# Three gathers in flight instead of two between two expert layers

## The reference

```
routed = sum over the 6 chosen experts k of  w[token, k] * expert_k(norm(x))[token]
x = x + routed + shared(norm(x))                       # layer 0 mixture
idx, w = small products of norm(x); s = sum(g[idx] * w) # lookup
x = x + s * (column sums of W_out) + b_out
probs = softmax(norm(x) @ gate_w.T); top 2 experts per token, then that mixture
```

## Time and profile before

| | us |
|---|---|
| median of three runs | 896.84 (895.16 to 898.3) |
| the profiled execution's own time | 900.07 |
| its span, first to last instruction | 898.3 |
| PE busy | 686.2 (76%) |
| DVE busy | 639.4 (71%) |
| ACT busy | 453.0 (50%) |
| POOL busy | 438.7 (49%) |
| DMA_INDIRECT of L1373, the gathers, 96 | 95.1 busy, 49.8 idle before them |

### The profile page before, as it was taken

How to read it: one execution, slowest core, us unless ns; L and a number is a source line. 1 busy time by engine, 2 the same in 40 slices (tenths; PEclk the granted TensorE clock), 3 DMA queues, 4 the chain that set the end, 5 groups by cost and what they waited for, 6 DMA issues and landing times.

```text
span 898.3 us, 17392 instructions
## 1 busy us (share of the span) xinstructions
PE 686.2 (76%) x5945; PEld 405.3 (45%) x5945; DVE 639.4 (71%) x1333; ACT 453.0 (50%) x620; POOL 438.7 (49%) x674
## 2 busy tenths in 40 slices
PE   4799999999999999714989999615244541899992
PEld 2422223223222233303889997312213311799991
DVE  5899998999899989862767643548688863344442
ACT  4778887888888888501434443101011011455550
POOL 4140002361255216576767774677766664255552
PEclk9999999999999999956999999955555555899997
DMA  7999999999999201253977663111111110133336
GB/s 243 290 319 282 314 295 297 311 296 287 273 341 367 119 3 50 69 140 103 271 231 211 168 176 100 45 42 46 55 57 39 52 58 26 33 52 50 53 44 156
DMA packets 83479, 142.91 MB, mean 159 GB/s; under 512 B 10736, under 2 KB 75728, under 8 KB 81888
## 3 DMA queue, kind: packets, MB, share of 16 engines
q1 hardware_dynamic: 57744, 118.07, 44.2%
q0 software_dynamic: 12784, 17.40, 8.1%
q10 hardware_dynamic: 12864, 6.33, 2.5%
HBM read 116.57 MB, written 101.34 MB: 243 GB/s over the span
## 4 chain that ended last, share of the span: by engine, by line
PE 55%; DMA 14%; DVE 10%; issue 7%; POOL 6%; ACT 6%; SPq 2%; POOLq 0%; ACTq 0%; DVEq 0%
PE PS L641 13%; DMA GB<-y_scratch,slotc 8%; PE PS L626 7%; PE PS L968 7%; PE PS L615 7%; PE PS L978 3%; PE PS L779 3%; ACT PB L1102 3%; PE PS L766 3%; PE PS L768 3%; DMA XP<-slots_scratch 3%; POOL slots_scratch L1316 2%; PE PS L754 2%; POOL slots_scratch L1391 2%; DVE routed L1767 1%
## 5 line engine op out<-in xcount | busy, mean ns | idle before, releaser
L1613 DVE TENSOR_SCALAR PS<-PS 128x1024 f32<-128x1024 f32 x244 | 289.6, 1228 | 14.1 <-PE PS L615 10.1
L1102 ACT ACTIVATE PB<-PS 128x1024 f32<-128x1024 f32 x224 | 227.8, 1025 | 46.8 <-PE PS L626 40.1
L641 PE MATMUL PS<-PB,VS 128*32 128x256 f32 x2048 | 164.2, 393 | 0.1
L1373 POOL DMA_INDIRECT GB<-y_scratch,slotc x96 | 95.1, 991 | 49.8 <-DMA GB<-y_scratch,slotc 34.8
L1316 POOL DMA_INDIRECT slots_scratch<-XN,slot x96 | 92.8, 967 | 52.8 <-ACT PB L1102 29.3
L615 PE MATMUL PS<-QS,KP 64*128 64x512 bf16 (+1 forms) x576 | 98.9, 359 | 9.0 <-ACT PB L1102 6.0
L626 PE MATMUL PS<-QM,KP 64*128 64x512 bf16 (+1 forms) x576 | 100.1, 362 | 2.2 <-DVE PS L1613 2.1
L1417 POOL DMA_INDIRECT sums_scratch<-YO,XG x39 | 60.7, 1556 | 60.0 <-DVE YO L1981 57.2
L968 PE MATMUL PS<-XTT,WB 128*128 128x128 f32 x624 | 77.8, 279 | 0.0
L968 PEld LDWEIGHTS PS<-XTT,WB 128*128 128x128 f32 x624 | 74.6, 196 | 0.1
L626 PEld LDWEIGHTS PS<-QM,KP 64*128 64x128 bf16 x576 | 25.1, 93 | 103.8 <-issue 49.9
(11 more groups left out here) (289 smaller groups left out, 1316.3 us busy)
## 6 DMA issues: line engine op xcount, KB each, us to landing
y_scratch<-YP SPq DMA_DIRECT2D x80, 128.0 KB, 2.3
slots_scratch<-slots_scratch SPq DMA_DIRECT2D x1, 8768.0 KB, 32.7
W0GU<-in_w0gu SPq DMA_DIRECT2D x1, 6144.0 KB, 48.1
XP<-slots_scratch ACTq DMA_DIRECT2D x80, 64.0 KB, 2.6
XP<-slots_scratch SPq DMA_DIRECT2D x80, 64.0 KB, 2.6
W1GU<-in_w1gu SPq DMA_DIRECT2D x8, 512.0 KB, 3.9
W0D<-in_w0d SPq DMA_DIRECT2D x1, 3072.0 KB, 16.8
XG<-slots_scratch SPq DMA_DIRECT2D x39, 68.5 KB, 1.9
```

Source lines behind the costliest of these rows:

```text
L641: last = mm(PS[32 * j:32 * j + 32, at:at + HALF], VS[:, n, g * HG + j, :], PB[u // 2 % 3][:, 2 * (j % 2) + j // 2, q], start=(n == 0 and h ...
L1102: A(PB[u // 2 % 3][:, 2 * hp:2 * hp + 2, :], pair_banks(u).rearrange("p (j q) -> p j q", j=2), ACT.Exp).then_inc(sem("exp_done"), 1)
L1373: gp.indirect_dma_start(GB[:, t, k, :], None, y0_dram.rearrange("b p d -> (b p) d"), bass.IndirectOffsetOnAxis(ap=slotc[:, t, k:k + 1], ax ...
L1613: TS_(pair_banks(u), pair_banks(u), 4.0, 0.0, ALU.mult, ALU.max).then_inc(sem("relu_done"), 1)
```

## The change

One constant. The semaphores `gathered0`, `gathered1` become `gathered0`, `gathered1`, `gathered2`; gather g waits for gather g - 3; `combined` waits on three semaphores with 2 gathers of each tile on each, instead of two with 3 on each. Nothing else differs.

```
-        IN_FLIGHT = 2
+        IN_FLIGHT = 3
...
                     if g >= IN_FLIGHT:
                         pool.wait_ge(sem(f"gathered{g % IN_FLIGHT}"), 16 * (g // IN_FLIGHT))
...
                 for g in range(IN_FLIGHT):
                     dve.wait_ge(sem(f"gathered{g}"), 16 * (TOP0 // IN_FLIGHT) * (t + 1))
```

## The result

The changed kernel takes 890.05 us (median of 7 runs, 887.54 to 893.88) against 896.84 for the kernel before (7 runs, 894.5 to 900.23): 6.8 us less, a ratio of 0.9919 with a 95% interval of 0.99 to 0.9939. Run once more beside the last experiments it gave 892.4 against 900.98, 0.9909 (0.9884 to 0.9934). The forecast was 891.0, in a range of 887.5 to 895.8.

A forecast was written before the change was run, and what follows sets the result against it. POOL's gathers were taken to set the ends of stretches A and B, DVE those of C and D. Gains of 3.3 + 2.5 = 5.8 us off the median 896.84 gave 891.0 us, range 887.5 to 895.8.

The forecast's parts named there:

- The price of a gather: On POOL between the expert layers: 1.245 us (0.942 held plus 0.30) with three in flight, against 1.365 with two.
- the rival by which landings stretch: Gathers land one behind another, landings stretch to 4 us, pace stays 1.365: 896.8 us; chance 0.08.
- A: First stretch between expert layers, 45.37 us, ending at DVE's wait for POOL's factor; 30 gathers, 3.3 us gain, range 1.6 to 5.1.
- B: Second stretch, 36.65 us, also ending with DVE waiting for POOL's factor; 24 gathers, 2.5 us gain.
- C and D: Third and fourth stretches, 37.97 and 36.12 us; POOL waits for DVE's moments at their ends, so no gain.
- The stall of 1.62 us at the 18th gather: In A at 581.40: POOL idles 1.92 us in place of 0.30 on nothing visible; the extra 1.62 was kept.
- four tosses against L1766: In A, gathers starting together with DVE's L1766 may be held, 0.8 to 0.9 us each; two hits of four taken.
- The step-through: POOL's gathers in B followed against L1766 in the times of before: 3.1 or 1.9 us earlier, 3.7 with no hit.
- the first rival: Other two-input DVE instructions also hold gathers, all four hits in A: gain 1.5 to 2.5 us, 894.8; chance 0.14.
- the toss: In B the 18th gather starts 0.08 us ahead of an L1766 and may slip by or be held.
- The slower rival: Gathers hold DVE's L1766, 12 of them, 0.7 us each: 8.4 us lost against 5.8 gained, 899.4; chance 0.06.
- the prediction's best case: No gather held in A or B: 5.1 + 3.7 = 8.8 us gained, 888.0; chance 0.14 as a rival.

The follow-up runs named there:

- the last experiments: Changed kernel with four gathers of chunk 2, in place of six, ahead of the last pair of scalings of B: 891.01 us against 900.98 for the kernel before.

## Why the prediction was right

- **The price of a gather** (1.245 for 1.365 us) and **the landing** that doesn't grow (2.5): as forecast; the rival by which landings stretch fell with the first profile. A landing was felt once after all, the longest of 3.8, for 0.57 us of idle time in D, where POOL has time to spare.
- **Which stretches pay**: A and B pay, C and D don't. The run with three in flight for C and D alone (1.0006) shows it, where the shares of the chain of waits would have promised 5 us.
- **A: 3.3 forecast, 6.2 measured**, more than the 5.1 that the prediction gave for no hit at all. Two terms were mis-sized. The stall of 1.62 us at the 18th gather was kept, as if it belonged to that gather; it runs from a landing, and with three in flight most of it is hidden. And of four tosses against L1766 two hits at 0.85 were counted, where one gather was held by 0.44: 1.26 less. 3.3 + 1.62 + 1.26 = 6.2. The tosses themselves were misread: only the last L1766 of A, at 586.60, began with a landing, and the gather that started 0.1 us ahead of it slipped by. The other three began right behind L1757, which waits for PE, so it is the pace of PE and DVE that decides which gather they meet; the one of 573.57 began inside the second of them. POOL's row beside the last L1766, then DVE's rows:

```profile
586.50 0.94 POOL L1373 DMA_INDIRECT GB<-y_scratch,slotc  x1 [0.30 <-issue]
```

```profile
572.58 0.69 DVE L1757 TENSOR_TENSOR X<-X,PS 128x512 f32<-128x512 f32 x1 [3.28 <-PE PS L815]
573.18 0.95 DVE L1766 TENSOR_TENSOR GB<-GB,wtok 128x768 f32<-128x768 f32 x1
...
586.60 0.96 DVE L1766 TENSOR_TENSOR GB<-GB,wtok 128x768 f32<-128x768 f32 x1 [3.15 <-DMA GB<-y_scratch,slotc]
```

- **B: 2.5 forecast, 1.8 measured** between these two profiles, and 2.9 against the 37.7 of the other profiles with two in flight. The step-through had two held gathers (B 3.1 shorter) or three (1.9 shorter), and 2.5 lies between. Four were held: L1837, which had not been counted, held the 16th for 0.47, and with that the 18th, the toss, began 0.52 inside its L1766. This is the first rival in part, at a price of one hit more in B; in A, where that rival had all four gathers held, one was.
- **The slower rival**, gathers that hold DVE: L1766 at 925 to 978 ns against 925 to 1017 shows none of it. Short instructions such as L1801 do, by 0.1 to 0.2 us each, but DVE's busy time in C and D grew by no more than 0.17 and 0.09, where the rival had 8.4 us.
- **The sum** came near with some luck. By the stretches of the two profiles 7.7 went where 5.8 was forecast: A gave 2.9 more, B 0.7 less, and C and D took back 0.25 that had been put at nothing. The medians moved by 6.8, and by 8.6 the second time, which is just inside the 8.8 of the prediction's best case.

## What to carry to other kernels

Before a queue is made deeper, divide the landing by the issue time: here 2.5 + 0.28 over 1.245 is 2.2, so two was just short, three is enough, and six gives nothing. Then ask at the end of each stretch who waits for whom: a wait in the middle of a stretch whose end another engine sets is worth nothing, however large its share in the chain of waits. Once an issuing engine is the bound, the order of its list is the next thing to try: two gathers moved out of B made that stretch 2.1 us shorter, though the whole time does not show it clear of its scatter.

## What the runs showed of the hardware

- A gather whose issue begins well inside a DVE instruction with two SBUF inputs (0.05 us or more after its start, 0.15 or more before its end) ends 0.81 to 0.85 us after that instruction, in every case in the twelve traces. One that begins 0.1 us ahead of L1766 is not held, and L1766 beside it takes 0.96, as alone. The Trainium skill, page "SBUF — State Buffer", section "SBUF: two separate sides", has the lock on the shared port pair that fits the first half; its whole-instruction lock for whichever comes first is not borne out for L1766 here, which stayed below 980 ns in the changed kernel.
- DVE is not free of gathers, though: L1801, with one tensor as input, took 0.43 in place of 0.22 where it lay across the end of a gather, and ended 0.06 after it.
- From the landing that POOL waited for to the start of its 114th indirect DMA 1.62 us passed in all ten traces in which it can be seen, against 0.26 elsewhere, wherever that DMA stood. With one or two in flight this is a stall of 1.4 to 1.7 us, with three 0 to 0.45, and in the one trace with six none.
